# Placing the query strips of an attention stage by ScalarE transfers instead of TensorE matmuls

## The reference, cut to what matters

```python
qh = (q @ Wq.T)... ; kh = (k @ Wk.T)... ; vh = (v @ Wv.T + bv)...
scores = jnp.einsum('bhsd,bhtd->bhst', qh, kh) * scale   # then the row's maximum is taken off, exp, times vh, divided by the sum
```

## Time and profile before

| what | value |
|---|---|
| executions without a profile | 990.39, 996.11, 999.69 us |
| the profiled execution | 1008.2 us, its span 1006.4 us |
| PE busy, of the span | 781.2 us (78%), mean granted clock 0.88 of 2.4 GHz |
| DVE busy | 541.2 us (54%) |
| ACT busy | 415.6 us (41%) |
| POOL busy | 395.6 us (39%) |

### The profile page before, as it was taken

The page is one execution under the profiler, slowest core; times in us unless marked ns, Lnnn a source line. Parts: engine busy times, 40 slices in busy tenths (PEclk is TensorE's granted clock), DMA queues, the critical chain, the costliest instruction groups (busy, mean ns, idle before and its releaser), DMA issues.

```text
span 1006.4 us, 16757 instructions
## 1 busy us (share of the span) xinstructions
PE 781.2 (78%) x5254; PEld 589.3 (59%) x5254; DVE 541.2 (54%) x1770; ACT 415.6 (41%) x745; POOL 395.6 (39%) x462
## 2 busy tenths in 40 slices
PE   6687167984889657658885666799788999989797
PEld 4576156874788535547774445687445555555564
DVE  6544122321437324535793234465777888888585
ACT  3433023542465222324432112243345555555586
POOL 5435734023610461563004545601566644445300
PEclk9589677997899776779897778899999999999799
DMA  9492236773312220631021231201345444544011
GB/s 304 143 310 74 83 91 186 229 244 101 108 51 67 81 54 21 245 105 32 22 64 56 57 98 46 58 21 62 99 117 140 133 121 119 161 118 116 7 32 53
DMA packets 95532, 106.38 MB, mean 106 GB/s; under 512 B 12612, under 2 KB 70340, under 8 KB 94039
## 3 DMA queue, kind: packets, MB, share of 16 engines
q1 hardware_dynamic: 76472, 78.95, 25.0%
q0 software_dynamic: 8608, 18.22, 7.2%
q10 hardware_dynamic: 10368, 8.13, 2.9%
HBM read 69.07 MB, written 36.18 MB: 105 GB/s over the span
## 4 chain that ended last, share of the span: by engine, by line
PE 53%; another core or an unknown queue 15%; DVE 14%; issue 9%; ACT 4%; POOL 3%; DMA 1%; SPq 0%; DVEq 0%; ACTq 0%; POOLq 0%
PE y_ps L1893 6%; PE y_ps L2020 5%; PE hid_ps L1881 4%; PE y_ps L2112 3%; PE hid_ps L2005 2%; PE hid_ps L1871 2%; PE hid_ps L2088 2%; PE hid_ps L2100 2%; PE hid_ps L2089 2%; PE tr_ps L2168 2%; PE hid_ps L1989 2%; PE hid_ps L1872 2%; PE hid_ps L1873 2%; PE hid_ps L1991 1%
## 5 line engine op out<-in xcount | busy, mean ns | idle before, releaser
L1262 DVE SCALAR_TENSOR_TENSOR zb<-hid_ps,w,sg 128x128 f32<-128x128 f32 x280 | 78.6, 344 | 89.9 <-ACT sg L1636 43.5
L1154 DVE COPY yo<-y_ps 128x256 f32<-128x256 f32 x76 | 31.6, 415 | 171.0 <-remote 84.1
L654 POOL DMA_INDIRECT xr<-b_tokens,idx_sb x70 | 67.5, 964 | 135.7 <-DVE idx_sb L915 90.3
L1893 PE MATMUL y_ps<-plain,hT 128*128 x624 | 93.2, 298 | 16.5 <-issue 14.3
L1893 PEld LDWEIGHTS y_ps<-plain,hT 128*128 128x128 f32 x624 | 85.5, 212 | 19.3 <-issue 19.2
L663 POOL DMA_INDIRECT yg<-a_rows,idx_a x64 | 60.9, 952 | 89.7 <-DMA a_rows<-yo 49.2
L1317 DVE TENSOR_REDUCE negmax<-hid_ps 128x4 f32<-128x512 f32 x128 | 85.4, 682 | 6.8 <-PE hid_ps L2089 5.9
L1552 ACT ACTIVATE zb<-hid_ps 128x512 f32<-128x512 f32 x78 | 46.4, 595 | 102.9 <-PE hid_ps L1873 60.5
L1881 PE MATMUL hid_ps<-ident,zb 128*128 128x128 f32 x312 | 52.3, 295 | 46.1 <-ACT zb L1552 37.8
L2005 PE MATMUL hid_ps<-ident,zb 128*128 128x128 f32 x280 | 47.9, 299 | 46.3 <-issue 29.7
L2020 PE MATMUL y_ps<-staged,hT 128*128 x560 | 82.1, 295 | 0.0
(11 more groups left out here) (353 smaller groups left out, 1894.2 us busy)
## 6 DMA issues: line engine op xcount, KB each, us to landing
region<-k_strips SPq DMA_DIRECT2D x128, 64.0 KB
region<-k_strips SPq DMA_DIRECT2D x32, 256.0 KB
region<-hl SPq DMA_DIRECT2D x128, 64.0 KB
k_strips<-k_halves SPq DMA_DIRECT2D x24, 256.0 KB
region<-nought SPq DMA_DIRECT2D x6, 1024.0 KB
a_rows<-yo SPq DMA_DIRECT2D x20, 256.0 KB
b_rows<-yo SPq DMA_DIRECT2D x18, 256.0 KB
k_halves<-region SPq DMA_DIRECT2D x16, 256.0 KB
```

Source lines behind the costliest of these rows:

```text
L654: g.indirect_dma_start(xr[:, q % 3, j * RB:j * RB + w], None, src, bass.IndirectOffsetOnAxis(ap=rows.bitcast(U32), axis=0)).then_inc(x_til ...
L1262: ins = v.scalar_tensor_tensor(zb[:, m % 2, es], hid_ps[1 + m % 2][:, es], w4[:, (QA + q) % 3, j, e:e + 1], sg[:, m % 2, es], op0=ALU.mult ...
L1893: t.matmul(y[:, c0:c0 + P], hT[:, n % 2, cs], w2a[:, bass.ds(e * FA + c * P, P)], start=c == 0, stop=False)
```

## The change

What it does, part by part:

- **Query strips by transfers.** `place`, its two matmuls a step on PE and the ACT copy to `qp` are gone. The rows of a strip are now interleaved (row 4 j + r holds part r of head value j), and a strip is filled by three transfers of 32 rows by 2 KB from `headh`, `headl`, `headh`. For steps 0 to 3 SP issues them (12 transfers) after its last store of stage B's rows; for step tau + 4 ACT issues two after `osb` and the third after `weights(tau, 3)`. PE's `scores(s, 0)` waits for all three (`q_in`), and ACT's copy into `headh` waits for all strips of the block before. POOL clears the four `qp` buffers once, after the last up-projection of stage B.
- **Key strips stored directly.** `k_halves` and `lay_k` are gone: SP stores the halves in three strided transfers into `k_strips`, so 24 copies and 16 stores become 24 stores.
- **Maxima in PSUM.** `negmax` moves from SBUF into the free bank `cb_ps`.
- The small product with the last layer's bias moves from tau = 25 to tau = 30, into `hid_ps[0]`, with the wait for it at stage D's first matmul.

```diff
-        negmax = sb("negmax", [P, 2, NT, HG])
+        negmax = cb_ps[:, 0:2 * NT * HG].rearrange("p (s b h) -> p s b h", s=2, b=NT)
...
-                sp.dma_start(k_half[0, rows, :], k_hi[i % 2].bitcast(F32)).then_inc(k_st[i % 2], 16)
-                sp.dma_start(k_half[1, rows, :], k_lo[i % 2].bitcast(F32)).then_inc(k_st[i % 2], 16)
+                strips = k_img[b * SG * P:(b + 1) * SG * P, :].rearrange("(p r) c -> p r c", r=4)
+                for r, half in enumerate((k_hi, k_hi, k_lo)):
+                    sp.dma_start(strips[:, r, :], half[i % 2].bitcast(F32)).then_inc(k_st[i % 2], 16)
...
+            sp.wait_ge(c_sel, 1)
+            sp.wait_ge(c_ql, 1)
+            for s in range(QPS):
+                for r, half in enumerate((headh, headl, headh)):
+                    sp.dma_start(qp[s][r:P:4, :].bitcast(F32), half[s * 32:s * 32 + 32, :].bitcast(F32)).then_inc(q_in[s], 16)
             sp.wait_ge(w_sel, weights_done(QA + QB - 1))
-            sp.wait_ge(b_up, NBT)
             load_v(0)
...
-            g.memset(flat(place).bitcast(F32), 0.0).then_inc(c_sel, 1)
...
+            pool.wait_ge(b_up, NBT)
+            g.memset(region2[:, 2 * BT:(2 + QPS) * BT].bitcast(F32), 0.0).then_inc(c_sel, 1)
...
-                link(v.tensor_copy(nmpad[:, :, :, 3 * HD], negmax[:, s % 2]))
-                v.tensor_tensor(nmpad[:, :, :, 3 * HD + 1], negmax[:, s % 2], nmpad[:, :, :, 3 * HD], ALU.subtract).then_inc(c_nm, 1)
+                link(v.tensor_copy(nmpad[:, :, :, 0, 3], negmax[:, s % 2]))
+                v.tensor_tensor(nmpad[:, :, :, 1, 3], negmax[:, s % 2], nmpad[:, :, :, 0, 3], ALU.subtract).then_inc(c_nm, 1)
...
+            def place_q(s, r):
+                if QPS <= s < STEPS:
+                    if s % SG == 0:
+                        eng.wait_ge(c_ql, s // SG + 1)
+                    eng.wait_ge(c_qs, s - QPS + 1)
+                    half = headl if r == 1 else headh
+                    a.dma_start(qp[s % QPS][r:P:4, :].bitcast(F32),
+                                half[s % SG * 32:s % SG * 32 + 32, :].bitcast(F32)).then_inc(q_in[s % QPS], 16)
...
-                if 0 <= tau + 4 < STEPS:
-                    eng.wait_ge(c_plq, tau + 5)
-                    if tau >= 0:
-                        eng.wait_ge(c_qs, tau + 1)
-                    a.activation(qp[(tau + 4) % QPS], cb_ps[:], ACT.Copy).then_inc(c_qp, 1)
+                place_q(tau + 4, 0)
+                place_q(tau + 4, 1)
                 if 0 <= tau < STEPS:
                     weights(tau, 2)
                     weights(tau, 3)
+                place_q(tau + 4, 2)
...
                         eng.wait_ge(c_pq, b + 1)
+                        for k in range(QPS):
+                            eng.wait_ge(q_in[k], 48 * b)
                         a.activation(headh, y_ps[1][:], ACT.Copy).then_inc(c_qh, 1)
...
-                    eng.wait_ge(c_qp, s + 1)
+                    eng.wait_ge(q_in[s % QPS], 48 * (s // QPS + 1))
...
-                if 0 <= tau + 4 < STEPS:
-                    if tau >= -3:
-                        eng.wait_ge(c_qp, tau + 4)
-                    if tau % SG == 0:
-                        eng.wait_ge(c_ql, tau // SG + 2)
-                    if tau == 26:
-                        eng.wait_ge(c_folds, 6)
-                    place_heads(tau + 4)
```

More of the change, by code:

```diff
@@ L150, in build @@
         wch, wcl = part(region1, 54, 2 * P, 2, P), part(region1, 55, 2 * P, 2, P)
-        place = region1[:, 28 * BT:30 * BT].rearrange("p (w g r) -> p w g r", w=2, g=SG)
         headh, headl = part(region1, 30, BT), part(region1, 31, BT)
@@ L246, in build @@
         diag_clear = sem("diag_clear")
-        kv_mm, kv_hi, kv_lo, v_st, k_done = (sem(n) for n in ("kv_mm", "kv_hi", "kv_lo", "v_st", "k_done"))
+        kv_mm, kv_hi, kv_lo, v_st, k_ones = (sem(n) for n in ("kv_mm", "kv_hi", "kv_lo", "v_st", "k_ones"))
         k_st = [sem(f"k_st{k}") for k in range(2)]
@@ L256, in build @@
         c_pq, c_qh, c_ql, c_sel, c_folds = (sem(n) for n in ("c_pq", "c_qh", "c_ql", "c_sel", "c_folds"))
-        c_plq, c_qp, c_mask = (sem(n) for n in ("c_plq", "c_qp", "c_mask"))
+        c_mask = sem("c_mask")
+        q_in = [sem(f"q_in{k}") for k in range(QPS)]
         c_s1, c_max, c_nm, c_nmt, c_qs = (sem(n) for n in ("c_s1", "c_max", "c_nm", "c_nmt", "c_qs"))
@@ L537, in _ @@
                     sp.wait_ge(diag_clear, 16 * (KDS + QDS))
-                    sp.wait_ge(k_done, 16 + 48 * NB)
+                    sp.wait_ge(k_ones, 16)
+                    for k in range(2):
+                        sp.wait_ge(k_st[k], 48 * (NB // 2))
                     for k in range(3):
@@ L763, in _ @@
                 gather_slots(q)
-            pool.wait_ge(a_down, NA)
-            g.memset(flat(place).bitcast(F32), 0.0).then_inc(c_sel, 1)
-            pool.wait_ge(c_sel, 1)
-            heads = ident[:].rearrange("p (h d) -> p h d", d=HD)
-            for which, copies in enumerate(((0, 2), (1,))):
-                rows = place[:, which].rearrange("p g (j r) -> p (g j) r", j=HG)
-                for r in copies:
-                    g.tensor_copy(rows[:, :, r * HD:(r + 1) * HD], heads).then_inc(c_sel, 1)
+            pool.wait_ge(b_up, NBT)
+            g.memset(region2[:, 2 * BT:(2 + QPS) * BT].bitcast(F32), 0.0).then_inc(c_sel, 1)
             pool.wait_ge(w_sel, weights_done(QA + QB - 1))
@@ L1676, in _ @@
                     a.activation(headh, cb_ps[:], ACT.Copy).then_inc(c_qh, 1)
-                elif T == 34:
-                    eng.wait_ge(c_plq, 1)
-                    a.activation(qp[0], cb_ps[:], ACT.Copy).then_inc(c_qp, 1)
             def weights(s, b):
@@ L2027, in _ @@
             eng.wait_ge(a_hh, NA)
-            def place_heads(s):
-                g = s % SG
-                t.matmul(cb_ps[:], place[:, 0, g, :], headh, start=True, stop=False)
-                t.matmul(cb_ps[:], place[:, 1, g, :], headl, start=False, stop=True).then_inc(c_plq, 1)
             slots_T_first(QA, 0)
@@ L2123, in last_block_use @@
                     eng.wait_ge(x_updated, C0 + (tau - 7) // SG + 2)
-            eng.wait_ge(c_sel, 5)
+            eng.wait_ge(c_sel, 2)
             for tau in range(-3, STEPS + 3):
@@ L2138, in _ @@
                     for b in range(NT):
-                        ins = t.matmul(tr_ps[:, b * P:(b + 1) * P], nmpad[:, b].rearrange("p h r -> p (h r)"), ident16[:],
+                        ins = t.matmul(tr_ps[:, b * P:(b + 1) * P], nmpad[:, b].rearrange("p h d r -> p (h d r)"), ident16[:],
                                        start=True, stop=True)
@@ L2184, in _ @@
                     t.matmul(y_ps[0][:, 0:1], raw[:, raw_slot(NRAW_B), P:2 * P], bv, start=True, stop=True).then_inc(c_folds, 1)
-                if tau == 25:
-                    eng.wait_ge(c_qp, tau + 5)
+                if tau == 30:
                     eng.wait_ge(c_folds, 4)
+                    eng.wait_ge(c_max, NT * STEPS)
                     for c in range(CD):
-                        ins = t.matmul(cb_ps[:, c:c + 1], fc1[:, c * P:(c + 1) * P].bitcast(F32), beta, start=True, stop=True)
+                        ins = t.matmul(hid_ps[0][:, c:c + 1], fc1[:, c * P:(c + 1) * P].bitcast(F32), beta, start=True, stop=True)
                     ins.then_inc(c_folds, 1)
@@ L2227, in up_d @@
                     eng.wait_ge(xTl_ready, NB + b + 1)
+                if b == 0 and c == 0:
+                    eng.wait_ge(c_folds, 6)
                 if b:
```

34 lines of the change are left out of this document (8 added, 26 removed).

## The result

The changed kernel took 1021.24 us (median of 4 runs, 1014.4 to 1026.1) where the kernel before, run beside it, took 997.65: ratio 1.022, 95% interval 1.018 to 1.026. It is 24 us slower. The forecast was 1022 us, slower.

What follows compares the result with a forecast made beforehand. PE was taken as the bound in attention, DVE a close second. Steady steps 19, steps 3 to 6 3 or 4, seam 1.4 and keys -2 gave +26 us on the 996.11 median: 1022 us, range 1005 to 1050.

Steps and rivals of the forecast that it cites:

- The ring: Attention: last line 2100, exponential, third issue, landing, next step's first matmul, fourth quarter, line 2100 again; 8.0 us against 7.19.
- the shorter ring: Attention step with the skill's fixed 2.0 us per DMA and an issue of 0.33: 0.25 us shorter, estimate 1015 us.
- the steady steps: Attention steps 7 to 31: 24 steps at 8.0 us instead of 7.19, +19 us.
- rival 1: Attention strips landing under DMA load, taking the 3.6 us upper bound: +28 more, 1050 us; chance 0.16 for 1036 to 1055.
- Rival 3: Attention: PE's clock falls to 1.2 GHz in half of the 28 steps, +48, so 1070 us; chance 0.07.
- Rival 2: Attention strips come in time because ACT issues the third transfer early; 31 x 0.58 = -18, 977 us; chance 0.08.
- Rival 4: Stage A: its 13.70 us wait goes with the key copies, -14 in place of -2, 1010 us; chance 0.10.
- Steps 3 to 6: Attention's first steps with ACT-placed strips: 33.9 us instead of 29.67, so +4.
- The seam: From stage B to attention: step 0 starts 4.5 us late for its strips, mostly covered, so +1.4 us.
- Keys -2: Key strips stored directly, fewer copies and issues between 152 and 254 us: -2 us, bounds -14 and +2.
- Maxima 0: Attention's maxima in PSUM: line 1326 falls to its fast time, off the path; 0, bounds -3 and +3.
- ScalarE's wait for its copy to `headh`: Attention: the copy waits for the third transfer of a block's last step; DVE's maximum 0.4 us late, costing nothing.

Runs made afterwards that it cites:

- e7: Kernel before, still placing strips by matmuls, with ScalarE also issuing the changed kernel's 84 strip transfers into a slot nothing reads: 818.1 us, ratio 1.0066 to the kernel before.
- e1: Changed kernel with the third strip transfer issued right behind the first two: 818.5 us, ratio 1.0066 to the kernel before.
- e2: Changed kernel with all three strip transfers issued between the exponentials of quarters 0 and 1: 824.2 us, ratio 1.0138 to the kernel before.
- e3: Changed kernel with the third strip transfer split into two of 32 KB, places unchanged: 862.1 us, ratio 1.063 to the kernel before.
- e6: Changed kernel with three steps' strips in four placed a step further ahead, each transfer waiting only for its half: 818.4 us, ratio 1.0070 to the kernel before.
- the other chip: The changed kernel itself, run again on a chip with shorter first two stages: 839.5 us, ratio 1.034 to the kernel before.
- e4: Changed kernel with the maxima back in SBUF: 839.9 us, ratio 1.034 to the kernel before.
- e9: e8 with the seam's twelve strip transfers issued by two engines: 991.9 us, ratio 1.0025 to the kernel before.
- e11: e9 with the strip issues spread, one to a gap between ScalarE's instructions: 987.9 us, ratio 1.0019 to the kernel before.
- e5: Kernel before with only the key strips stored directly, query strips still placed by matmuls: 811.6 us, ratio 1.000 to the kernel before.
- e8: e6 with the three issues behind ScalarE's block copies instead of ahead of them: 1000.0 us, ratio 1.0105 to the kernel before.
- e10: e8 with the maxima in SBUF: 994.1 us, ratio 1.0036 to the kernel before.

## Why the prediction was right, and where not

**The mechanism was right.** The first matmul of each later step waits for the third strip, which is issued with the last exponential. e7 shows that a wait for a landing costs, not the load by itself; e1, e2, e3 and e6 that the wait follows the place of the issue.

**The ring was mis-sized, and slow steps made up for it.** Predicted 8.0 us for every step; the plain one took 7.28. Of its terms, 0.45 and 0.43 came out as 0.44 and 0.43. First to fourth quarter took 4.28 (830.39 to 834.67), not 4.48. From the begin of the exponential to the issue it took 0.07 us and from there to the first matmul 2.06, where I had 2.65 for issue, landing and semaphore: I had added an issue's duration to a landing that counts from the begin of the issue. Together 4.28 + 0.44 + 0.43 + 0.07 + 2.06 = 7.28. Over the 84 transfers on the other chip the landing took 2.0 us at least, 2.2 in the median and 3.7 at most (the trace above gives none). The Trainium skill, DMA: Bandwidth & Descriptors, "Anatomy of one DMA — SWDGE (gpsimd) path", has about 2.0 us fixed, for transfers that GpSimd issues; ScalarE's 2.0 to 2.2 us agree with it, and the shorter ring that I worked out beside it was nearer to the plain step. By blocks at full clock, the steady steps would have cost 24 x (7.57 - 7.19) = +9 us and not +19. The other 8.1 us of the measured 17.1 are in the four blocks with a dip. Three steps in them (from 745.10, 862.51 and 901.95) took 5.77, 6.63 and 5.70 us from first to fourth quarter, where plain ones take 4.3: 5.1 us for the clock. One strip that landed late, rival 1 below, is another 2.5. So the mechanism was right, but the total came out right by luck, by two errors of opposite sign.

**Rival 3, the clock,** was put at 0.07 as a case of its own, +48 us. It came in part, in more than half of the blocks and by 0.02 to 0.09. One of my own conditions for "wrong" was a clock under 0.95 in attention; it was 0.94 from step 0 at 689.30 to 943 us and 0.95 from 697 on, where the kernel before had 0.99 and 0.98. What I had against it, 5 us of dense work between the waits, didn't rule it out. The dips stand in single steps, behind a long wait:

```profile
745.10 0.40 PE L2072 MATMUL hid_ps<-maskq,ident 128*128 128x512 bf16 x1 [2.61 <-DMA region<-region]
...
747.26 0.63 PE L2072 MATMUL hid_ps<-maskq,ident 128*128 128x512 bf16 x1
...
750.87 0.38 PE L2072 MATMUL hid_ps<-maskq,ident 128*128 128x512 bf16 x1
```

The matmul that takes 0.38 us at the 2.4 GHz level takes 0.63 at 747.26, and 0.38 again at 750.87; over the stretch from first to fourth quarter the granted clock was 0.70. In the two profiles of the changed kernel, here and on the other chip, nine of the 56 waits for a strip were over 2.1 us, and behind each of the nine the quarters ran at 0.57 to 0.72; of the 47 shorter waits two were followed by a dip (1.82 us at 901.95, 2.03 at 699.93 on the other chip). In e3 four waits of 2.38 to 2.71 us were followed by none, so what sets a dip off isn't shown by the length of the wait alone. The price was 1.3 to 2.3 us for such a step, not the 3.4 that I had put on it. The Trainium skill, TensorE: Matmul & The Clock Gate, "HAM oscillation — how this bites in real kernels", has the clock fall for waits on DMAs between groups of matmuls, for each group; the trace agrees for the long waits and not for the rest.

**Rival 1, landing under load,** didn't come as a rule. From issue to first matmul it took 2.7 to 3.1 us in four more steps (from 711.43, 736.79, 822.45 and 918.29) and over the 3.6 us of my upper bound once: beside SyncE's loads for the last stage the strip issued at 857.78 us was waited for until 862.51:

```profile
855.22 0.43 SPq L478 DMA_DIRECT2D yg<-d_scales_in  x1
855.69 0.91 SPq L409 DMA_DIRECT2D raw<-d_fc_in  x2
...
857.78 0.48 ACTq L1680 DMA_DIRECT2D region<-region  x1
...
862.51 0.61 PE L2072 MATMUL hid_ps<-maskq,ident 128*128 128x512 bf16 x1 [3.13 <-DMA region<-region]
...
862.57 0.60 ACT L1726 ACTIVATE region<-y_ps 128x512 fp32r<-128x512 f32 x1 [4.20 <-DMA region<-region]
```

It is no accident of one execution: the same step waits 2.96 us on the other chip and 3.31 in e4, and e7's wait of 6.27 us stands there too. That SyncE's loads are the cause is argued, not shown; no run moves them.

**Rival 2, strips in time,** I priced at 977 us: the placing matmuls' 18 us would be gained. e6, e9 and e11 have the strips in time and stand at 1.007, 1.003 and 1.002. This price was wrong. PE was 26.7 us busy in a block of 28.7, so I took it for the bound; with 2.3 us of it gone the block at full clock gets 0.2 us shorter at first (27.6 in e9 against 27.8 for the same steps before), and 0.9 in e11. What PE is spared it spends waiting. Over steps 7 to 31 it was busy 13.7 us less in e6 than in e5, and idle 13.4 us more: 11.7 us against 5.3 behind VectorE's halves and sums for the block, 5.0 against 2.8 for its maxima, 3.5 against 1.2 for GpSimd's mask, the rest in small pieces.

**Rival 4, stage A relieved,** didn't come. The medians of the result differ by 23.6 us, and from the end of stage B on the kernel lost 23.0 in the profiles, which leaves nothing for stage A. In e8, e9 and e10, whose keys are stored directly too, a wait of 10.1 to 13.6 us still stands at 221 to 226 us where the kernel before had its 13.70. e5 can't tell, since on its chip there is no such wait.

**The smaller terms.** Steps 3 to 6: +4 predicted, +3.0 and +4.0 on the two chips. The seam: step 0 9.0 us behind stage B's last work where it was 5.4, so 3.6 late (4.5 predicted), of which 0.7 is left at step 3 (1.4 predicted). Keys -2: 0 in e5, within 2 us. Maxima 0: 0 in e4; line 1326 went from 604 to 229 ns, and the Trainium skill's rule on two SBUF inputs (SBUF — State Buffer, "Who interferes with whom") agrees with all 32 of them. ScalarE's wait for its copy to `headh`, 12.9 us in six places, was counted as nothing: the step behind such a copy, from 830.39, is the plain one of 7.28 us. After step 31 I predicted 0: +2.2 here and 0.1 on the other chip. Here that step's quarters took 5.66 us at a granted clock of 0.72, 4.48 before, which is 1.2 of it; the rest stays open. "All four steps alike" and "PE busy 0.7" missed: 0.82 of the time in a block at full clock.

**What stays open.** What, besides the length of a wait, makes the clock dip in one step and not in the next of the same code. And why the first two blocks of e9 take 29.9 and 30.6 us at full clock where its later ones take 26.9 to 28.1; the kernel before has 29.6 there in its trace, and e5 28.1 on the other chip.

## What to carry to other kernels

A transfer that takes over an engine's work has to be issued over 2 us ahead of its reader, on an engine whose next instruction isn't wanted soon: each issue is some 0.5 us in which the instruction behind it doesn't begin, and three in a row are an exponential late. Look for the last event that an issue stands behind in its queue, and follow that event back; if the reader is on that path, the kernel has a ring, and its length is the step. A wait on that path can cost more than its length: behind those of over 2.1 us the next step took 1.3 to 2.3 us longer. And before counting on the instructions that a change takes off the busiest engine, ask what that engine will wait for next: here 2.3 us a block came off PE and 0.2 to 0.9 arrived.

## What the runs showed of the hardware

An SBUF to SBUF transfer of 64 KB, issued by ScalarE in 0.48 us at best, lands 2.0 us after its issue begins at best and 2.2 to 2.6 in the median of a kernel; the first matmul that waited for it began 4.7 us behind the issue at most in the changed kernel (857.78 to 862.51). One issue (0.48 us at 835.61) ran beside ScalarE's activation ahead of it (0.60 us at 835.54); three in a row (1.79 us in e2) held the next exponential up by 1.30. A VectorE subtraction of 128 x 16 elements from two SBUF operands took 607 ns in the median beside GpSimd's work (e4), and 229 with one of them in PSUM, in all 32 of its instances; the maxima's reductions took 691 ns into PSUM (e6) and 682 into SBUF (e5). TensorE's granted clock was 0.57 to 0.72 over the four quarters behind each strip wait of over 2.1 us in the changed kernel, on both chips, and 1.00 behind 45 of the 47 shorter ones. Two chips of the same kind ran stages A and B of the changed kernel in some 511 and 689 us: on the second, "another core or an unknown queue" holds 14% of the chain of waits, on the first nothing.
